# A graph layer with a routed feed-forward layer: the scatters of the last chunk but one stand eleven gathers sooner in Pool's list, and nine tiles' fetches and one store stand ahead of the last scatters

## The reference

```python
x = x + _L0_gnn_ref(_layernorm(x), src, dst, W, b)
#   xw = features @ W;  msg = xw[edge_src] * norm_src[edge_src]
#   agg = segment_sum(msg, edge_dst);  relu(agg * norm_dst + b)
x = x + _L0_ffn_ref(_layernorm(x)[None], Wr, br, ln_g, ln_b, W1, b1, W2, b2)[0]
#   probs = softmax(xt @ Wr + br);  top 2 experts, their weights made to sum to 1
#   h = gelu(xe @ W1[e] + b1[e]);  y = h @ W2[e] + b2[e];  out = sum of the two weighted y
```

## Time and profile before

| | us |
|---|---|
| runs | 1611.21, 1613.84, 1607.22; median 1611.21 |
| the profiled execution, its own time | 1615.5 |
| its span in the trace | 1613.9 |
| busy: PE, DVE, ACT, Pool | 1165.9, 1026.4, 644.6, 1157.6 |
| granted TensorE clock, mean | 0.85 of full speed |

### The profile page before, as it was taken

How to read it: one execution, slowest core, us unless ns; L and a number is a source line. 1 busy time by engine, 2 the same in 40 slices (tenths; PEclk the granted TensorE clock), 3 DMA queues, 4 the chain that set the end, 5 groups by cost and what they waited for, 6 DMA issues and landing times. The chain is left out here.

```text
span 1613.9 us, 27049 instructions
## 1 busy us (share of the span) xinstructions
PE 1165.9 (72%) x9182; PEld 993.0 (62%) x9182; DVE 1026.4 (64%) x2810; ACT 644.6 (40%) x1273; POOL 1157.6 (72%) x1087
## 2 busy tenths in 40 slices
PE   6961657664761849879699696968949877898870
PEld 6961536452541838768588585856848766777760
DVE  8995767687682765847557575774756567556640
ACT  3974332133201424434245252423414453555660
POOL 8885777777777777777777777777777707677523
PEclk9999756576665979989899898987979999999995
DMA  8359878767667578787787787767768768899990
GB/s 279 116 180 341 295 257 277 256 223 238 227 190 253 172 243 275 219 257 239 229 271 242 254 260 221 241 224 234 227 207 248 233 183 248 231 286 280 306 284 8
DMA packets 258142, 381.53 MB, mean 236 GB/s; under 512 B 24339, under 2 KB 217479, under 8 KB 253780
## 3 DMA queue, kind: packets, MB, share of 16 engines
q1 hardware_dynamic: 192280, 232.69, 44.1%
q0 software_dynamic: 59360, 140.70, 30.1%
q10 hardware_dynamic: 6364, 6.40, 1.2%
HBM read 302.58 MB, written 80.08 MB: 237 GB/s over the span
## 5 line engine op out<-in xcount | busy, mean ns | idle before, releaser
L914 POOL DMA_INDIRECT gt<-zt,srcI x768 | 787.7, 1026 | 244.0 <-issue 179.5
L1313 PE MATMUL ps<-gt,S 128*128 128x257 f16 x1536 | 297.6, 318 | 181.0 <-DMA gt<-zt,srcI 168.0
L1431 PE MATMUL ps<-xe,w1b 128*128 128x256 f16 (+1 forms) x2736 | 332.0, 275 | 27.5 <-DVE xe L1891 18.5
L1313 PEld LDWEIGHTS ps<-gt,S 128*128 128x128 f16 x1536 | 190.9, 152 | 243.0 <-DMA gt<-zt,srcI 215.2
L1260 ACT ACTIVATE h<-ps,cb 128x256 f32<-128x256 f32 (+1 forms) x456 | 224.9, 543 | 283.9 <-PE ps L1431 270.6
L1446 PE MATMUL ps<-w2b,hT 128*128 128x256 f16 x2544 | 305.1, 278 | 14.8 <-DVE yb L1926 5.9
L1431 PEld LDWEIGHTS ps<-xe,w1b 128*128 128x128 f16 x2736 | 260.7, 102 | 70.6 <-DVE xe L1891 26.8
L1446 PEld LDWEIGHTS ps<-w2b,hT 128*128 128x128 f16 x2544 | 252.9, 100 | 51.1 <-issue 14.4
L1898 DVE SCALAR_TENSOR_TENSOR hT<-h,cb,hT 128x512 f16<-128x512 f32 (+1 forms) x228 | 161.0, 711 | 132.8 <-ACT hT L1264 130.5
L1264 ACT ACTIVATE hT<-h,cb 128x512 f16<-128x512 f32 (+1 forms) x228 | 157.8, 692 | 7.4
L943 POOL DMA_INDIRECT xs<-xrow,slI x98 | 100.9, 1030 | 74.1 <-DVE slI L1634 44.6
(11 more groups left out here) (292 smaller groups left out, 1493.3 us busy)
## 6 DMA issues: line engine op xcount, KB each, us to landing
w1b<-ws SPq DMA_DIRECT2D x57, 1024.0 KB, 6.6
w2b<-ws SPq DMA_DIRECT2D x57, 1024.0 KB, 8.8
ws<-w2b SPq DMA_DIRECT2D x16, 1024.0 KB, 5.6
xb<-xs SPq DMA_DIRECT2D x49, 260.0 KB, 8.3
gt<-zt,srcI POOLq DMA_INDIRECT x768, 5.3
ys<-yb SPq DMA_DIRECT2D x34, 256.0 KB, 9.4
zg<-zf SPq DMA_DIRECT2D x8, 1028.0 KB
gt<-zg SPq DMA_DIRECT2D x8, 1028.0 KB
```

Source lines behind the costliest of these rows:

```text
L914: e.indirect_dma_start(out=gt[:, i % NG, :], out_offset=None, in_=zt, in_offset=bass.IndirectOffsetOnAxis(ap=srcI[:, c, r:r + 1].bitcast(u ...
L1313: inst = e.matmul(PS[r % 2][:, 0:257], S[:, r % NS, :, c], gt[:, i % NG, part * 257:part * 257 + 257], start=(c == 0 and part == 0), stop= ...
L1431: inst = e.matmul(UP[n % 2][:, z * BS:z * BS + 128 * size(m)], w[:, l, kk, j * 128:(j + 1) * 128], xe[m % 2][:, k, kk, 0:128 * size(m)], s ...
```

## The change

`scatters(c)` is taken out of the second stage of `send_stages`. For chunk 8 it becomes a chain of the first stage, beside the route ("r1", "r3", "r5"), and may be placed once "r1" is placed (`begun`). For the other chunks nothing changes. cg 0 to cg 8 (`arg >= NC - 1` is still held) and the first give may be placed ahead of the scatters of chunk 9. A cc waits until the route of chunk 9 is placed (`s["placed"] <= LAST`). The planner's costs and gaps for cg, sums and give are other numbers, and after the last scatters a cg is placed only where it doesn't push a give or sums back. `...` marks what is left out of the diff.

```diff
+def scatters(c):
+    return [("xs", (c, j), (("POOL", 2.56),)) for j in range(CHUNKS[c][1] - CHUNKS[c][0])] + [("sent", c, ())]
 def send_stages(c):
     yield [[("r1", c, (("DVE", 3.6),)), ("r3", c, (("PE", 0.6), ("ACT", 0.4))), ("r5", c, (("DVE", 3.2),))],
-           [xr(max(g for g in range(NGR) if GROUPS[g][0] == c))]]
-    yield [[("xs", (c, j), (("POOL", 2.56),)) for j in range(CHUNKS[c][1] - CHUNKS[c][0])] + [("sent", c, ())],
+           [xr(max(g for g in range(NGR) if GROUPS[g][0] == c))]] + ([scatters(c)] if c == LAST - 1 else [])
+    yield ([scatters(c)] if c != LAST - 1 else []) + [
...
-        if max(s["chain"], s["base"]) > s["now"] or clock["POOL"] > s["now"] + 2.6 or LAST not in sent:
+        if max(s["chain"], s["base"]) > s["now"] or clock["POOL"] > s["now"] + 2.6 or LAST not in sent and s["given"]:
             return False
...
-            emit("sums", b, (("POOL", 1.3 * (SUMS[b][1] - SUMS[b][0])),), s["now"])
+            emit("sums", b, (("POOL", 2.0),), s["now"])
             s["summed"] += 1
+            s["chain"] = clock["POOL"] + 13.0
...
-            emit("give", gives[0], (("POOL", 1.7 * GIVES[gives.popleft() - M0]),), s["now"])
+            k = GIVES[gives[0] - M0]
+            emit("give", gives.popleft(), (("POOL", 1.9 * k),), s["now"])
             s["given"] += 1
+            s["chain"] = clock["POOL"] + (5.0 if k > 1 else 2.6)
...
-        s["chain"] = clock["POOL"] + 5.0
...
-                if kind == "cg" and (clock["POOL"] > s["now"] + 2.5 or LAST not in sent):
+                if kind == "cg" and (clock["POOL"] > s["now"] + 2.5 or LAST not in sent and arg >= NC - 1):
+                    continue
+                if kind == "cc" and s["placed"] <= LAST:
+                    continue
+                if kind == "cg" and (gives or batches) and LAST in sent and max(clock["POOL"], s["now"]) + 2.6 > max(s["chain"], s["base"]) + 1.5:
                     continue
...
+                if kind == "xs" and arg[0] == LAST - 1 and arg[0] >= s["begun"]:
+                    continue
...
+                if kind == "r1":
+                    s["begun"] = arg + 1
...
-                chain.at = end + 2.0 if kind == "cg" else s["now"] + 4.0 if kind in ("pl", "pw") else s["now"] + 1.5 if kind == "blanks" else s["now"] if kind == "xs" else end
+                chain.at = end + 5.0 if kind == "cg" else s["now"] + 4.0 if kind in ("pl", "pw") else s["now"] + 1.5 if kind == "blanks" else s["now"] if kind == "xs" else end
```

More of the change, by code:

```diff
@@ L189, in plan @@
     clock = {"PE": 0.0, "DVE": 0.0, "ACT": 0.0, "POOL": 0.0}
-    s = {"now": 0.0, "bank": 0.0, "held": {}, "free": {}, "norms": -1, "nT": 0, "nW": 0, "hh": 0, "xr": 0, "placed": 0, "tabled": 0, "read": -1, "routed": -1, "loaded": 0, "asked": False, "given": 0, "base": 1e9, "late": 1e9, "summed": 0, "chain": 0.0,
+    s = {"now": 0.0, "bank": 0.0, "held": {}, "free": {}, "norms": -1, "nT": 0, "nW": 0, "hh": 0, "xr": 0, "placed": 0, "begun": 0, "tabled": 0, "read": -1, "routed": -1, "loaded": 0, "asked": False, "given": 0, "base": 1e9, "late": 1e9, "summed": 0, "chain": 0.0,
          "pb": 0, "pe": 0, "pG": 0, "ps": 0, "pz": 0, "ph": 0, "po": 0, "pw": 0, "wj": 0, "zl": 0, "zat": 1e9}
```

## The result

The changed kernel takes 1604.01 us in the median of 20 runs, the kernel before 1611.61 us beside it (20 runs): a ratio of 0.9953, with a 95% interval of 0.994 to 0.9965. So it is faster by 7.6 us, 0.47%. The forecast was 1597, a gain of 14.2 us: about half of that came, and the time lies 7 us above the forecast and inside the range (1581 to 1608). The prediction drew the bound between faster and the same at 1603.2 us. The median is 0.8 us above it, so by that bound the result is "the same", although the interval leaves out a ratio of 1. The profiled execution took 1603.62 us with a span of 1602.1. A ratio leaves out executions over 1.5% above the shortest of their kernel, so further down it need not be the ratio of the medians beside it. In two later groups of runs every kernel took 200 us longer, and there the gain was gone; the experiments come to that.

The account below looks back on a forecast made before the run. Pool's chain of landings was taken to bound the end. From chunk 9's scatters its gives and sums ran to a last give at 1592.1; plus 7.4 gave a 1599.5 span, minus 2.7 a median of 1597 us, range 1581 to 1608.

Parts of the forecast that it names:

- What bounds: End of kernel: Pool's backlog of landings, not PE; last give issued 27.7 us after the blocks end, forecast 19 us.
- Chunk 8's scatters: Scatters moved to 1260.92, ahead of 15 fetches: wait 1.2 us, last fetch 1.0 us later, last add unchanged at 1298.
- Rival 3: Chunk 9's scatters come too late, waiting on block 33's store and Pool, so PE pays: slower, 1616 us; chance 0.05.
- Store of block 33: On SP behind `w1b` of block 36: issued at 1310, landing 10.3 us, so the first gather starts at 1320.3.
- Nine tiles and give 34: 18 gathers and a give ahead of chunk 9's scatters: 27.7 us of issue, scatters at 1348.0, Pool 14.7 us ahead net.
- PE and the 13 us: Chunk 9's scatters start 13.0 us later, but block 38's first up comes at 1370.5, so PE pays only 1.4 us.
- The chain: Pool's gives and sums after chunk 9's scatters, from 1358.5: pairs 9.3 us each, last give 1592.1, span 1599.5.
- From span to median: Last step of the sum: median taken 2.7 us below the span, as in the kernel before; 1599.5 becomes 1597.
- Rival 1: Gives land quicker than 9.57 us a pair, Pool meets the blocks and they bind the end: 1579 to 1585; chance 0.26.
- Rival 2: Landings of sums, pairs and halves at the end take longer, adding 10 us to the chain: 1607 us; chance 0.13.
- Rivals 3 and 4: The third as above; the fourth: nine fetches don't fit before chunk 9's scatters, only swap places; near 1609, chance 0.06.
- The rule that spoke against the rows: Skill page estimates 2.3 us for one tile's give; trace rows show 3.19 unloaded, 6.86 loaded. By the page, blocks end last.

Follow-up runs that it names:

- the gap: Kernel before with only the rule letting nine tiles' rows be fetched ahead of the last chunk's scatters, old planner numbers: 1829.18 us (1.0033), then 1814.48 us (0.9998).

## Why the prediction was right, and where it was off

**What bounds.** Pool's chain, not the blocks: borne out by the changed kernel (16.6 us between last block and last give) and by the run without the last sums, where six pairs are released by blocks instead of landings and the time falls. Block 40 was 14.6 us later, and each step of the chain behind the last scatters still came within 3.4 us of its forecast.

**Chunk 8's scatters.** Wait 1.2 us forecast, 2.30 measured; start 1262.1, measured 1262.76; last fetch 1290.5, measured 1291.27; last add 1298, measured 1296.50. Right on the first machine, and the value of zero for the end was borne out there by both runs that take it apart. I counted no loss on the way from the last add to chunk 9's slots, and it grew by 3 us, which the 18 gathers covered. What I had not weighed was that the wait has no margin: with 1.2 us as my price I named no condition under which it is ten times that, and no rival had this mechanism. Rival 3 looked for the danger at the last scatters, and the new wait came at those of chunk 8.

**Store of block 33.** Issue at 1310, measured 1307.28 and right behind `w1b` of block 36 as forecast. From there to the first gather 10.3 us were forecast, 6.75 measured. So the gather is 6.3 us sooner than forecast, at 1314.03. Its row names no releaser. But in all eleven profiles of kernels with the gap the first gather comes 6.1 to 7.0 us behind the store's issue, wherever that is, so the store is what it waits for.

**Nine tiles and give 34.** 27.7 us forecast, 27.59 measured (1314.03 to 1341.62). Scatters of chunk 9 at 1348.0, measured 1341.62.

**PE and the 13 us.** First up of block 38 at 1370.5, measured 1367.03 in PE's timeline, against 1369.15 before: no loss there. But PE lost later, by DVE's waits, and I had the blocks' end at 1573 where it is 1576.8 (1576.45 + 0.35); within the ends that I gave.

**The chain.** From the scatters' end to sums 0: 27.9 forecast, 31.3 measured (1352.24 to 1383.54). Sums 0 to sums 3: 107.9 and 109.3. So half of the 6.3 us went in the first three pairs, and sums 3 is at 1492.85 for 1494.3. Behind it: 16.5 for its landing, 18.15 measured; five pairs 46.5, measured 49.10 (9.82 each instead of 9.3); seven halves 34.8, measured 33.33; the tail 7.4, measured 8.67. The span is 1602.1 for 1599.5. The terms under load were each priced somewhat low, by 4.3 us for the sums and the five pairs together: the 9.57 of the earlier trace rows was a better value than my 9.3, and 9.8 is what came.

**From span to median.** This is the step that was furthest off. I took the median as 2.7 us below the span, because the profiled execution of before was 1615.5 and its median 1611.2. But that execution was simply a slow draw; that of after (1603.62) lay at its own median (1604.01), 1.9 us above its span. The difference from profile to profile is 11.8 us (1613.9 - 1602.1), and that from median to median 7.6. Of the 7.0 us between forecast and result, 2.6 are the chain and 4.6 this step (less 0.2 of rounding).

**The rivals.** Rival 1 didn't occur: landings stayed at 9.8 a pair. Rival 2 occurred in small, 4.3 us of its 10. Rivals 3 and 4 did not on the first machine. In the later groups the result is slower by 0.4 and 0.6%. To slower I had given a chance of 0.06, by a mechanism (scatters of chunk 9 that wait for the store and Pool) that is not the one seen: there they wait for their slots.

**The rule that spoke against the rows.** The landings of after are again longer than the estimate of 2.3 us by the Trainium skill, page "DMA: Bandwidth & Descriptors", section "Anatomy of one DMA — SWDGE (gpsimd) path". With the weights in, the chain that ended last has the landing of give 55 at 2.73 us and those of the three before it at 3.18 to 3.70, and from issue to issue give 55 takes 3.5 us (1.56 of issue, 1.93 idle). A pair under load takes 9.82. The measurement decides, and Pool didn't catch up.

**Which part made the gain.** My sum gave it to the 18 gathers that leave the busy stretch. The runs show it more sharply: neither the scatters (first machine, 0.9995), nor the numbers (first machine, 0.9998), nor the gap (later groups only, 1.0033 and 0.9998) moves the time by itself. The fetches in the gap together with the numbers do (0.9947). What the gap alone is worth on the first machine was not run, and in the later groups the whole change gains nothing either, so that the two need each other is shown for one side only: the numbers need the gap.

## What to carry to other kernels

Where a serial chain of landings binds the end, ask of each edit whether it takes a step out of the chain's whole stretch: a step that only changed places with another, or stood closer to it, gave nothing here, even where the last sums came 16 us sooner. A step placed by counting another engine's instructions, as the scatters ahead of eleven gathers here, holds as long as both engines keep their pace: its wait went from 2.3 us to 10.8 and more. If putting it back costs nothing, leave it where it has slack. And compare medians with medians: one profile stood 4 us above its own kernel's median, which was half of what there was to find.

## What the runs showed of the hardware

A pair of accumulating scatters from Pool (two tiles, 128 KB each) takes 9.8 us from issue to issue in the mean of five (9.2 to 10.5) while the DMA engines are loaded (share 1.06). The last sums, one accumulating transfer of eleven tiles (1408 KB), takes 14.6 to 20.3 us to the next give's issue over the twelve profiles that have it. In the changed kernel PE was busy through all of these 18.15 us, in the kernel before for 10.37 of 19.24, so a busier PE did not make it longer.

The second surprise is the whole machine. With the same bytes in the same DMA busy time and with instructions of ACT, DVE and Pool as long as ever, all kernels took 200 us longer in two of the four groups of runs. PE's share of that is 68.5 us of busy time at a granted clock of 0.81 instead of 0.85. A change worth -0.47% on one machine was worth +0.43% and +0.64% in those groups.
